# Attention edge pass on one core: sums moved up, one product and one mask moved between engines, GpSimd's scatters held

## The reference

```python
s_n, v_n = _equiv_layernorm(s, v, gamma_s, beta_s, gamma_v)
msg_s = (s_n @ Ws_src)[src] + (s_n @ Ws_dst)[dst]
msg_v = einsum(v_n, Wv_src)[src] + einsum(v_n, Wv_dst)[dst]
w1 = rbf @ W_rbf
m1_s, m1_v = _cg_tp(msg_s, msg_v, y0, y1, ...w1...)   # products with the edge row y
a = leaky(m1_s @ W_alpha) summed with alpha_dot       # 4 heads
amax = segment_max(a, dst);  ex = exp(a - amax[dst])
den = segment_sum(ex, dst);  alpha = ex / (den[dst] + 1e-16)
val_s = m1_s @ Ws_val
val_v = (m1_v @ Wv_val) * sigmoid(val_s @ Wg);  val_s = sigmoid(val_s)
m2_s, m2_v = _cg_tp(val_s, val_v, y0, y1, w2...)
agg = segment_sum(alpha * (m2 @ W_vlin), dst)
out = node + (agg_s @ Wps, agg_v @ Wpv)
```

## Time and profile before

| what | value |
|---|---|
| median of three runs | 4730.02 us |
| profiled execution, its own time | 4743.81 us |
| its span | 4742.0 us |
| granted TensorE clock, mean | 0.904 |
| TensorE, VectorE, ScalarE, GpSimd busy | 3709.4, 3285.3, 2442.6, 3346.5 us |
| edge pass of layer 1, first gather to last running maximum | 1132.8 to 2379.7 us |

### The profile page before, as it was taken

How to read it: one execution, slowest core, us unless ns; L and a number is a source line. 1 busy time by engine, 2 the same in 40 slices (tenths; PEclk the granted TensorE clock), 3 DMA queues, 4 the chain that set the end, 5 groups by cost and what they waited for, 6 DMA issues and landing times. The chain is left out here.

```text
span 4742.0 us, 73825 instructions
## 1 busy us (share of the span) xinstructions
PE 3709.4 (78%) x14102; PEld 1795.8 (38%) x14102; DVE 3285.3 (69%) x8309; ACT 2442.6 (52%) x7488; POOL 3346.5 (71%) x3644
## 2 busy tenths in 40 slices
PE   1999997775999999999910288888798789887665
PEld 0333334553333444444300133333566333333444
DVE  1566666774887898888868545554799455445999
ACT  0233324776555555555457534333699333333777
POOL 1566666997686787788546566666588567666888
PEclk9999998998999999999855589888899898988999
DMA  9222225886454554444379622222798222224886
GB/s 403 67 67 70 67 68 167 275 273 179 115 127 108 127 128 127 127 127 127 88 249 364 229 68 65 67 67 64 240 324 298 70 66 69 66 66 133 251 252 212
DMA packets 585572, 718.24 MB, mean 151 GB/s; under 512 B 79012, under 2 KB 409194, under 8 KB 585224
## 3 DMA queue, kind: packets, MB, share of 16 engines
q1 hardware_dynamic: 492812, 536.17, 37.6%
q0 software_dynamic: 86400, 142.71, 11.0%
q10 hardware_dynamic: 6268, 38.40, 2.0%
HBM read 488.77 MB, written 245.93 MB: 155 GB/s over the span
## 5 line engine op out<-in xcount | busy, mean ns | idle before, releaser
L548 POOL DMA_INDIRECT aggregates<-agg_out,scatter_index x600 | 613.9, 1023 | 402.9 <-issue 247.6
L1296 ACT ACTIVATE y_chunk<-residual,ln_minus_mean_rstd,ln_rstd 128x160 f32<-128x160 f32 x1568 | 701.4, 549 | 201.9 <-POOL ln_minus_mean_rstd L1369 140.9
L1365 POOL TENSOR_TENSOR ln_rstd<-ln_var_eps,minus_half 128x4 f32<-128x4 f32 x392 | 504.7, 1287 | 104.5 <-ACT ln_var_eps L1305 66.7
L531 POOL DMA_INDIRECT gathered<-x_layer,gather_index x400 | 393.3, 983 | 177.7 <-issue 116.5
L1260 PE MATMUL psum<-self_weights,x_chunk_T 128*128 128x160 f32 (+1 forms) x2352 | 414.5, 320 | 57.2 <-ACT x_chunk_T L1319 54.1
L624 PE MATMUL psum<-identity,scaled_x 128*128 128x128 f32 x600 | 146.1, 282 | 378.2 <-ACT scaled_x L570 352.9
L1461 DVE BATCH_NORM_STATS2 ln_stats<-residual 128x6 f32<-128x160 f32 x1568 | 390.5, 311 | 6.8
L1260 PEld LDWEIGHTS psum<-self_weights,x_chunk_T 128*128 128x128 f32 x2352 | 347.7, 192 | 93.3 <-ACT x_chunk_T L1319 53.5
L570 ACT ACTIVATE scaled_x<-gathered,sh_times_attr 128x160 f32<-128x160 f32 x400 | 138.4, 417 | 459.5 <-DVE sh_times_attr L681 305.3
L647 PE MATMUL psum<-hidden,weights 64*128 64x512 f32 x300 | 182.8, 692 | 187.8 <-ACT hidden L582 130.2
L531 POOL DMA_INDIRECT gathered<-in_x,gather_index x200 | 206.3, 1032 | 166.5 <-ACT scaled_x L570 79.2
(11 more groups left out here) (227 smaller groups left out, 10323.8 us busy)
## 6 DMA issues: line engine op xcount, KB each, us to landing
x_layer<-y_chunk SPq DMA_DIRECT2D x294, 320.0 KB, 4.7
x_chunk<-x_layer SPq DMA_DIRECT2D x294, 320.0 KB, 4.6
agg_chunk<-aggregates SPq DMA_DIRECT2D x196, 320.0 KB, 5.6
sh_rows<-in_sh_big SPq DMA_DIRECT2D x50, 768.0 KB
agg_chunk<-aggregates SPq DMA_DIRECT2D x98, 384.0 KB, 5.8
aggregates<-zero_rows ACTq DMA_DIRECT2D x1, 36864.0 KB
x_chunk<-in_x SPq DMA_DIRECT2D x98, 322.0 KB, 3.4
agg_chunk<-aggregates SPq DMA_DIRECT2D x98, 322.0 KB, 3.9
```

Of the source, the lines that this page charges most:

```text
L531: eng.indirect_dma_start(gathered[:, par, b, 0:width], None, x_table[l][:, :], bass.IndirectOffsetOnAxis(idx_src[:, par, b:b + 1], 0))\
L548: eng.indirect_dma_start(agg_table[:, :], bass.IndirectOffsetOnAxis(idx_last[:, q, b:b + 1], 0), agg_out[:, q, b, :], None, bounds_check=N ...
L1296: op = eng.activation(y_out[:, buf, b, :], res[:, buf, b, :], ACT.Identity, bias=shift[:, buf, b:b + 1], scale=rstd[:, buf, b:b + 1])
L1365: eng.tensor_tensor(rstd[:, buf, :], var_eps[:, q, :], minus_half[:, 0:T], ALU.pow)\
```

## The change

Four things move, all in layer 1's edge pass.

1. GpSimd: the row product and the segment marks leave its queue. Of its gathers, one tile's stands ahead of the scatters (two tiles' before), one tile's behind them ahead of rstd, and two tiles' behind rstd. The four scatters wait for the denominators' scan of the same step.
2. VectorE: the sums, their square and the row product stand at the head of the step, ahead of the denominators' scan; variance and epsilon right behind the vectors' scan; the apply behind the first two of the six message products; the reciprocal's addition behind the sixth.
3. ScalarE makes the segment marks, with one constant column more (`low_col`), so that the setup's count of constants goes from 7 to 8.
4. TensorE: the two HS products are 96 columns wide instead of 64; the rows 64 to 95 of the result are not read.

```diff
@@ setup @@
+        low_col = sb("segment_start_column", [128, 1])
-            eng.wait_ge(P["consts"], 7)
+            eng.wait_ge(P["consts"], 8)
+            eng.memset(low_col[:, :], -1e30).then_inc(P["consts"], 1)
@@ attn_gpsimd @@
-                    gather((0, 1))
+                    gather((0,))
                 if live(s, 6, NG):
                     g = s - 6
                     sem = S["scatter1"] if par else S["scatter0"]
                     eng.wait_ge(S["agg"], g + 1)
+                    if live(s, 4, NG):
+                        eng.wait_ge(S["den"], s - 4 + 1)
                     for b in range(T):
...
-                if live(s, 2, NG):
-                    a = s - 2
-                    eng.wait_ge(S["rows1"] if par else S["rows0"], (a - par) * 16 + 32)
-                    wait(eng, S["w_mm"], 6 * a)
-                    eng.tensor_tensor(z_rows[:, :], z_in[:, par, 0, :], z_in[:, par, 1, :], ALU.mult).then_inc(S["z"], 1)
                 if live(s, 0, NG):
-                    gather((2,))
+                    gather((1,))
...
                 if live(s, 0, NG):
-                    gather((3,))
-                if live(s, 3, NG):
-                    b_ = s - 3
-                    wait(eng, S["carried"], b_)
-                    eng.tensor_scalar(neg[:, :], goes_on[0:96, b_ * GE:b_ * GE + GE], -1.0, 1e30, ALU.add, ALU.mult)\
-                       .then_inc(S["neg"], 1)
+                    gather((2, 3))
@@ attn_scalar, between the tanh of the values and that of the gates @@
+                    wait(eng, S["carried"], g)
+                    eng.activation(neg[:, :], goes_on[0:96, bass.ds(g * GE, GE)], ACT.Identity, bias=low_col[0:96, 0:1],
+                                   scale=1e30).then_inc(S["neg"], 1)
@@ attn_tensor @@
-                    eng.matmul(pbank("HS", 64), X("Q1")[0:64, 0:64], q_y[0:64, 0, :], start=True, stop=False)
+                    eng.matmul(pbank("HS", 96), X("Q1")[0:64, 0:96], q_y[0:64, 0, :], start=True, stop=False)
...
-                    eng.matmul(pbank("HS", 64), X("HD")[0:96, 0:64], vy[:, 1, :], start=False, stop=True)\
+                    eng.matmul(pbank("HS", 96), X("HD")[0:96, 0:96], vy[:, 1, :], start=False, stop=True)\
@@ attn_vector, new head of the step @@
+                    for side, rows in enumerate((gathered, gathered_d)):
+                        op = eng.tensor_reduce(ln_sum[:, side, :], rows[:, q, :, 0:64], AX.X, ALU.add)
+                    op.then_inc(S["sums"], 1)
...
+                    eng.tensor_tensor(ln_sq[:, :, :], ln_sum[:, :, :], ln_sum[:, :, :], ALU.mult).then_inc(S["square"], 1)
...
+                    eng.tensor_tensor(z_rows[:, :], z_in[:, par, 0, :], z_in[:, par, 1, :], ALU.mult).then_inc(S["z"], 1)
@@ attn_vector, the six products @@
+                products(0, 2)
...apply of group s - 1
+                products(2, 6)
...addition and reciprocal of the denominators
```

More of the change, by code:

```diff
@@ L1040, in step @@
             def step(s, par):
+                if live(s, 1, NG):
+                    g, q = s - 1, 1 - par
+                    wait(eng, S["gather1"] if q else S["gather0"], (g - q) * 64 + 128)
+                    wait(eng, S["square"], g)
+                    for side, rows in enumerate((gathered, gathered_d)):
+                        op = eng.tensor_reduce(ln_sum[:, side, :], rows[:, q, :, 0:64], AX.X, ALU.add)
+                    op.then_inc(S["sums"], 1)
+                if live(s, 1, NG):
+                    g = s - 1
+                    eng.wait_ge(S["sums"], at(S["sums"], g + 1))
+                    wait(eng, S["variance"], g)
+                    eng.tensor_tensor(ln_sq[:, :, :], ln_sum[:, :, :], ln_sum[:, :, :], ALU.mult).then_inc(S["square"], 1)
+                if live(s, 2, NG):
+                    a = s - 2
+                    wait(eng, S["rows1"] if par else S["rows0"], (a - par) * 16 + 32)
+                    wait(eng, S["w_mm"], 6 * a)
+                    eng.tensor_tensor(z_rows[:, :], z_in[:, par, 0, :], z_in[:, par, 1, :], ALU.mult).then_inc(S["z"], 1)
                 if live(s, 4, NG):
@@ L1062, in step @@
                        .then_inc(S["scan_v"], 1)
-                if live(s, 5, NG):
-                    g, q = s - 5, 1 - par
-                    eng.wait_ge(S["rden"], at(S["rden"], g * 48 + 48))
-                    eng.wait_ge(S["scan_s"], at(S["scan_s"], g + 1))
-                    eng.wait_ge(S["scan_v"], at(S["scan_v"], g + 1))
-                    wait(eng, S["r_mm"], g)
-                    eng.tensor_tensor(o_s[:, :], sum_s[0:64, q, :], rden[0:64, :], ALU.mult).then_inc(S["o_s"], 1)
-                    eng.tensor_tensor(o_v[:, :], sum_v[:, q, :], rden[:, :], ALU.mult).then_inc(S["o_v"], 1)
-                if live(s, 1, NG):
-                    g, q = s - 1, 1 - par
-                    wait(eng, S["gather1"] if q else S["gather0"], (g - q) * 64 + 128)
-                    wait(eng, S["square"], g)
-                    for side, rows in enumerate((gathered, gathered_d)):
-                        op = eng.tensor_reduce(ln_sum[:, side, :], rows[:, q, :, 0:64], AX.X, ALU.add)
-                    op.then_inc(S["sums"], 1)
-                if live(s, 3, NG):
-                    g = s - 3
-                    eng.wait_ge(S["val"], at(S["val"], g + 1))
-                    eng.scalar_tensor_tensor(out=lk[0:64, :], in0=lk[0:64, :], scalar=0.2, in1=pbank("AV", 64),
-                                             op0=ALU.mult, op1=ALU.max).then_inc(S["leaky"], 1)
-                if live(s, 1, NG):
-                    g = s - 1
-                    eng.wait_ge(S["sums"], at(S["sums"], g + 1))
-                    wait(eng, S["variance"], g)
-                    eng.tensor_tensor(ln_sq[:, :, :], ln_sum[:, :, :], ln_sum[:, :, :], ALU.mult).then_inc(S["square"], 1)
                 if live(s, 1, NG):
@@ L1098, in step @@
                     eng.tensor_scalar(ln_var[:, :, :, :], ln_e2[:, :, :, :], EPS, None, ALU.add).then_inc(S["eps"], 1)
+                if live(s, 5, NG):
+                    g, q = s - 5, 1 - par
+                    eng.wait_ge(S["rden"], at(S["rden"], g * 48 + 48))
+                    eng.wait_ge(S["scan_s"], at(S["scan_s"], g + 1))
+                    eng.wait_ge(S["scan_v"], at(S["scan_v"], g + 1))
+                    wait(eng, S["r_mm"], g)
+                    eng.tensor_tensor(o_s[:, :], sum_s[0:64, q, :], rden[0:64, :], ALU.mult).then_inc(S["o_s"], 1)
+                    eng.tensor_tensor(o_v[:, :], sum_v[:, q, :], rden[:, :], ALU.mult).then_inc(S["o_v"], 1)
+                if live(s, 3, NG):
+                    g = s - 3
+                    eng.wait_ge(S["val"], at(S["val"], g + 1))
+                    eng.scalar_tensor_tensor(out=lk[0:64, :], in0=lk[0:64, :], scalar=0.2, in1=pbank("AV", 64),
+                                             op0=ALU.mult, op1=ALU.max).then_inc(S["leaky"], 1)
                 if live(s, 3, NG):
@@ L1106, in step, with products @@
                                                  op0=ALU.add, op1=ALU.mult).then_inc(S["qy"], 1)
[L1107 to L1119 removed]
+                def products(first, after):
+                    if live(s, 2, NG):
+                        g = s - 2
+                        eng.wait_ge(S["m_copied"], at(S["m_copied"], 2 * g + 2))
+                        wait(eng, S["vv_mm"], g)
+                        for k, (name, n, m) in list(enumerate((("B1", 128, m_s), ("B2", 128, m_s), ("C", 96, m_v),
+                                                               ("D", 96, m_v), ("F", 96, m_v), ("G", 96, m_v))))[first:after]:
+                            eng.wait_ge(S["w_mm"], at(S["w_mm"], 6 * g + k + 1))
+                            eng.tensor_tensor(pr[0:n, k, :], m[0:n, :], pbank(name, n), ALU.mult).then_inc(S["prods"], 1)
+                products(0, 2)
                 if live(s, 1, NG):
@@ L1127, in step @@
                     op.then_inc(S["applied"], 1)
+                products(2, 6)
+                if live(s, 4, NG):
+                    g = s - 4
+                    eng.wait_ge(S["den_t"], at(S["den_t"], g * 64 + 64))
+                    wait(eng, S["rec_out"], g * 16)
+                    eng.tensor_scalar(rec[:, :], den_t[:, :], 1e-16, None, ALU.add).then_inc(S["den_e"], 1)
                 if live(s, 4, NG):
```

21 lines of the change are left out of this document (4 added, 17 removed).

## The result

The changed kernel takes 4842.36 us (median of four runs, 4837.05 to 4849.73) against 4733.23 for the kernel before in the same runs: a ratio of 1.0226, 95% interval 1.0207 to 1.0244, so 2.3% slower. The forecast was 4762 with a range of 4697 to 4815. The direction was right, the size wrong by 80 us, outside the range. The profiled execution is the one of 4849.73 us (span 4847.9, mean granted clock 0.888).

The account below looks back on a forecast made before the run. A loop from the denominators' scan through GpSimd's rstd back to VectorE sets the step: 11.8 + 13.1 = 24.9 us, 0.74 more in 43 intervals, 32 us on 4730, so 4762 us, range 4697 to 4815.

Parts of the forecast that it names:

- The loop: Edge pass: denominators' scan, held GpSimd transfers, rstd, apply, VectorE's queue to the next scan; a step of 24.9 us.
- E to apply: From the denominators' scan end (E) through six GpSimd transfers and rstd to VectorE's apply: 11.8 us, between 10.5 and 12.7.
- The release of the wait 0.1: GpSimd's held scatter was to start 0.1 us after the denominators' scan ends.
- I take 1.3 in all: GpSimd transfers issued inside VectorE operations with two SBUF operands end late: 1.3 us a step, ends 0 and 1.7.
- Apply to E: VectorE's own queue from the apply to the next denominators' scan end: 13.1 us, give or take 0.1.
- the one more constant ... nothing: The added constant costs under 1 us at the start, behind the larger fills, so nothing.
- TensorE's width: HS product 96 columns wide: 1.0 us saved per step, worth nothing if TensorE then only waits longer.
- Clean loop: Rival: no collision and rstd at 2.95, a step of 23.5 to 23.9 us, 4702 to 4719 us; chance 0.17.
- no change: Rival: collisions of 0.3 to 0.7 us, a step of 23.9 to 24.3, within 10 us of 4730; chance 0.17.
- Hold not last: Rival: VectorE's own queue of 21.5 us decides the step, 130 us less, 4600 us; chance 0.08.
- TensorE's clock: Rival: TensorE's longer waits lower its clock, adding 48 us, 4810 us; chance 0.12.
- The SBUF rule: VectorE instructions with two SBUF inputs and GpSimd ones reading SBUF exclude each other; the waiting side resumes about 0.115 us later.

Follow-up runs that it names:

- no_hold: The changed kernel without the scatters' wait for the denominators' scan: 4668.1 us, ratio 0.9853 to the kernel before.
- hs64: The changed kernel, wait kept, with the two HS score products back at 64 columns: 4881.8 us, ratio 1.0303 to the kernel before.
- no_hold_zpool: The changed kernel without the scatters' wait and with the edge row product back on GpSimd: 4710.8 us, ratio 0.9947 to the kernel before.
- hold_alone: The kernel before with only the scatters' wait for the denominators' scan added: 4864.4 us, ratio 1.0266.
- hold_gathers: The changed kernel with the kernel before's buffer addresses and the wait moved behind the scatters, holding only the two second gathers: 4770.8 us, ratio 1.0016.

## Why the prediction was right in direction and wrong in size

The loop was the right mechanism: no idle time ahead of the denominators' scan, the vectors' scan at 1.25, the two products starting together, VectorE standing idle at the apply (1.9 to 4.0 us) in each of the 44 intervals that hold the wait. The step that failed is "E to apply: 7.5 + 1.3 + 2.95 + 0.05 = 11.8 us", with its end of 12.7. It measured 13.20 in the step shown, and rstd started at E + 10.1 (9.5 to 10.5 over the steps) where the prediction looked for 8.5 to 9:

- "The release of the wait 0.1" is 0.91 (2015.24 to 2016.15): 0.8 short, the largest term in the step shown. I took it from waits of compute instructions. The kernel before had the right row, which I hadn't read: a scatter released by ScalarE's copy that ends at 2401.57 starts at 2402.37, 0.80 later. no_hold's scatters show 0.80 to 0.85.
- "I take 1.3 in all" for collisions is 1.8: the four scatters and two gathers take 7.68 us where six free ones of 0.98 take 5.88. Since the release came 0.8 late, the second scatter was issued at 2017.47, where the scalars' scan ends and the vectors' scan begins, and it ended 0.8 us after the latter (2018.79): 2.13 us, 1.15 lost and not 0.85. The third takes 1.44 beside the outputs, which I had counted at nothing. Over the 44 intervals the collisions are 1.2 to 2.2 us, median 2.1: 0.8 above what I took, as much as the release, and above my upper end of 1.7.
- rstd at 2.96 was right; rstd to apply is 0.14, not 0.05.

From the first transfer's start to rstd's are 9.19 us where the sum had 7.42 + 1.3. That is 0.81 + 0.47 + 0.01 + 0.09 = 1.38 us on top of 11.82. Apply to E is 12.8 to 13.0 for a forecast of 13.1. A held step is 26.3 on average for 24.9, above the upper end of 25.8.

- **The sum.** (25.81 - 24.16) x 49 = 81 us in place of 32: 44 held intervals of 26.3, that is 94 more, and 13 less from the five that hold nothing, to which I gave no gain. About 14 more are the moved buffers, of which the prediction had "the one more constant ... nothing": its instruction is free, its address isn't. Between the two profiled executions some 11 remain: 6 us of a later start of the edge pass (its first gather at 1138.8 for 1132.8; 1131.1 to 1138.8 over the kernels, no cause shown) and what is within the spread of the runs.
- **TensorE's width** "is worth nothing if TensorE then only waits longer" was wrong: alone it saves 1.06% of the kernel before. The prediction calls L994 and L995 a pair of equal width, but their rows have 128 and 96 columns, and they too start 0.01 us apart. So equal width isn't what lets two products run together; that a product of 64 columns doesn't run beside one of 96, and one of 96 does, is all that was measured. Here the width's gain is inside the loop's idle time, but hs64 shows that it still keeps 39 us of clock loss away.
- **Clean loop and no change** (0.34 together) needed collisions under 0.7 us; there were 1.2 at the least. **Hold not last** (0.08): the queue without the wait came out at 22.3, not 21.5, since VectorE's products still wait 1.19 us for TensorE. Its time would have been 4655, not 4600.
- **TensorE's clock** (0.12): it is lower, 0.89 for 0.97, but follows the wait: without it the clock is 1.00. In the step shown VectorE waits for rstd after it has waited for TensorE, so what TensorE lost there cost nothing.

The SBUF rule that the prediction weighed (the Trainium skill, SBUF — State Buffer, section "SBUF: two separate sides") holds in its sense: a transfer issued in a scan is held. Its 0.115 us for going on isn't seen as such: the held transfer's instruction ends 0.8 us after the scan.

The whole sum: the moved sums, the product and the mask with the wider score product give 81 us (4737 to 4655.5), the wait takes 175 back (to 4830.6), the moved buffers 12.

## What to carry to other kernels

Before a wait is added to a queue, follow the loop that it closes: here everything behind the wait on GpSimd, rstd last, stood between one scan of VectorE and VectorE's own next input, so each microsecond of release and of collision was paid in 44 of the 49 intervals. Take the release of a waiting transfer from a row of a waiting transfer, not of a compute instruction. And when a change adds a buffer, check a stage that it doesn't touch; if that stage's transfers became slower, put the buffer where nothing moves.

## What the runs showed of the hardware

- A GpSimd indirect transfer that waits on a semaphore starts 0.8 to 0.9 us after its releaser ends: 0.80 to 0.84 behind ScalarE's copy in the kernel before, 0.90 to 0.92 behind VectorE's scan in the changed one, 0.80 to 0.85 in no_hold. rstd, a compute instruction of GpSimd, starts 0.09 us behind VectorE's variance (no_hold, 2013.18 to 2013.27).
- One that is issued as a VectorE scan of 1.25 us begins takes 2.13 us instead of 0.98 and ends 0.8 us after the scan, and a VectorE square of 128x8 beside a GpSimd product of 1.29 us takes 1.58 us instead of 0.17 (no_hold_zpool).
- Two TensorE products that use different halves of the rows start 0.01 us apart with 96 and 96 columns (2033.65 and 2033.66 us in the changed kernel) and with 128 and 96, but run one after the other with 64 and 96 (2.02 us for both in the kernel before).
- Four bytes more ahead of the node pass's buffers take its full DMA engines from 364 to 340 GB/s and the stretch from 276 to 294 us; 64 bytes do the same (342 GB/s, 292 us), 128 bytes don't (360 GB/s, 276 us).
- A wait of TensorE of 2.81 us was followed by 13 us at the 1.2 GHz level (granted clock 0.50) in hold_alone, one of 2.82 us by 12 us of it in hs64, one of 2.83 us by some 3 us of it in the changed kernel (the transposes, 2.79 us), and one of 1.10 us by 2.79 us of it in the kernel before.
- In hold_gathers ScalarE and VectorE, waiting for different products of TensorE, resumed 0.12 us apart, more than 6 us after both products' recorded ends. A long issue of SyncE (7.14 us) stood beside them; in the kernel before 26 of 48 such issues took 5.0 to 7.3 us and only three had such a wait of ScalarE beside them (3.6 to 4.6 us). No cause is shown.
